# Attention kernel: normalising each head before the output projection, with the softmax denominators inverted on 16 lanes and spread by transfers

## The reference, cut to what matters

```
q, k, v = qkv[0], qkv[1], qkv[2]            # (b, h, n, 64), q scaled by 64 ** -0.5
sim  = einsum('bhid,bhjd->bhij', q, k)      # causal mask on sim
attn = softmax(sim, axis=-1)
out  = einsum('bhij,bhjd->bhid', attn, v)   # (b, h, n, 64)
out  = transpose(out, (0, 2, 1, 3)).reshape(b, n, 16 * 64)
return out @ w_out                          # w_out: (1024, 128)
```

## Time and profile before

| | us |
|---|---|
| median of 3 runs | 1583.55 (1583.36 to 1583.85) |
| the profiled execution | 1578.72 |
| its span, first to last instruction | 1577.0 |
| PE busy | 1453.9 (92%) |
| DVE busy | 1076.1 (68%) |
| ACT busy | 1067.4 (68%) |
| POOL busy | 904.9 (57%) |
| granted TensorE clock, mean | 0.968 |

### The profile page before, as it was taken

One profiled execution on the slowest core, in us unless ns is written; L12 is line 12 of the kernel. 1 busy time (PEld: TensorE's weight loads), 2 busy tenths in 40 slices (PEclk: granted clock), 3 DMA queues, 4 the chain that ended last, 5 costly groups with the idle time before them and its releaser, 6 DMA issues.

```text
span 1577.0 us, 33357 instructions
## 1 busy us (share of the span) xinstructions
PE 1453.9 (92%) x9130; PEld 1128.0 (72%) x9131; DVE 1076.1 (68%) x2341; ACT 1067.4 (68%) x2590; POOL 904.9 (57%) x923
## 2 busy tenths in 40 slices
PE   3569999599999999999999999999999999999998
PEld 3458888477777777777777777777777777777776
DVE  6655555458866876687658776876687668766883
ACT  2536656277776777777767777777777777777775
POOL 0761000167665766676657666766676667666766
PEclk9669999699999999999999999999999999999999
DMA  8122111111111111111111111111111111111111
GB/s 308 48 83 72 52 58 48 40 38 38 33 28 41 38 33 28 41 38 33 28 39 40 33 28 39 40 33 28 39 40 33 28 40 39 33 28 41 37 28 54
DMA packets 58807, 72.86 MB, mean 46 GB/s; under 512 B 7400, under 2 KB 44560, under 8 KB 58640
## 3 DMA queue, kind: packets, MB, share of 16 engines
q1 hardware_dynamic: 40720, 52.57, 14.0%
q10 hardware_dynamic: 13824, 9.86, 2.0%
q0 software_dynamic: 4096, 8.40, 1.8%
HBM read 20.47 MB, written 16.52 MB: 23 GB/s over the span
## 4 chain that ended last, share of the span: by engine, by line
PE 67%; DVE 6%; issue 4%; ACT 3%; DMA 1%; SPq 0%; DVEq 0%; POOLq 0%; POOL 0%; ACTq 0%
PE max_ps L1291 9%; PE score_ps L1316 8%; PE score_ps L1317 8%; PE misc_ps L1350 8%; PE head_ps L1333 7%; PE head_ps L1337 7%; PE head_ps L1335 7%; PE misc_ps L1267 3%; PE max_ps L1294 2%; PE score_ps L1319 2%; DVE q_a L1125 2%; PE misc_ps L1261 2%; ACT p_hi L1082 1%; PE misc_ps L1300 1%; PE misc_ps L1263 1%
## 5 line engine op out<-in xcount | busy, mean ns | idle before, releaser
L1033 POOL TENSOR_TENSOR p_lo<-probs,p_hi 128x512 fp32r<-128x512 f32 (+3 forms) x768 | 773.7, 1022 | 432.0 <-ACT p_hi L1082 426.2
L1082 ACT ACTIVATE probs<-score_ps 128x512 f32<-128x512 f32 (+3 forms) x768 | 375.3, 489 | 250.8 <-PE score_ps L1319 170.9
L1135 DVE TENSOR_REDUCE row_max<-max_ps 128x1 f32<-128x128 f32 (+7 forms) x512 | 386.8, 756 | 171.6 <-PE max_ps L1294 161.0
L1082 ACT ACTIVATE p_hi<-score_ps 128x512 fp32r<-128x512 f32 (+3 forms) x768 | 373.1, 486 | 0.0
L1333 PE MATMUL head_ps<-p_hi,v_hi 128*65 128x512 f32 (+3 forms) x768 | 295.6, 385 | 0.3 <-POOL p_lo L1033 0.3
L1316 PE MATMUL score_ps<-q_a,k_a 128*128 128x512 f32 (+3 forms) x768 | 267.8, 349 | 14.0 <-issue 10.9
L1317 PE MATMUL score_ps<-q_b,k_b 65*128 65x512 f32 (+3 forms) x768 | 267.3, 348 | 0.0
L1291 PE MATMUL max_ps<-k_a,q_a 128*128 128x384 f32 (+5 forms) x768 | 250.1, 380 | 16.4 <-DVE row_max L1135 12.6
L1337 PE MATMUL head_ps<-p_lo,v_hi 128*65 128x512 f32 (+3 forms) x768 | 259.4, 338 | 0.0
L1335 PE MATMUL head_ps<-p_hi,v_lo 128*64 128x512 f32 (+3 forms) x768 | 259.0, 337 | 0.0
L1316 PEld LDWEIGHTS score_ps<-q_a,k_a 128*128 128x128 f32 x768 | 145.4, 189 | 60.0 <-issue 17.4
(11 more groups left out here) (170 smaller groups left out, 2105.6 us busy)
## 6 DMA issues: line engine op xcount, KB each, us to landing
k_a<-k_a SPq DMA_DIRECT2D x64, 256.0 KB, 3.8
q_b<-q_a SPq DMA_DIRECT2D x64, 256.0 KB, 4.3
sorted_x<-zeros SPq DMA_DIRECT2D x13, 384.0 KB, 16.1
w_raw<-sorted_x SPq DMA_DIRECT2D x26, 192.0 KB, 2.5
sorted_y<-result ACTq DMA_DIRECT2D x78, 64.0 KB, 1.6
acc<-in_L_attn_x_dram SPq DMA_DIRECT2D x4, 512.0 KB, 6.9
w_raw<-in_L_ffn_W_dram ACTq DMA_DIRECT2D x1, 2048.0 KB, 23.1
q_b<-shift SPq DMA_DIRECT2D x128, 2.0 KB
```

The lines of the kernel that those rows point to most:

```text
L1033: pool.tensor_tensor(p_lo[:, slot, 0:w], probs[:, slot, 0:w], p_hi[:, slot, 0:w].bitcast(F32), ALU.subtract).then_inc(p_split, 1)
L1082: ins = act.activation(p[:, (g * CH + c) % RING, 0:width], score_ps[(g * CH + c) % 2][:, 0:width], ACT.Exp, scale=SCALE)
L1135: dve.tensor_reduce(row_max[:, g % 2, t:t + 1], src, axes, ALU.max).then_inc(max_taken, 1)
```

## The change

Each head is now normalised before the output product, so that the two heads of a pair can share one product with 128 rows, and the denominator need not be carried through it. For each half of each group there is a chain (`CHAIN`, the numbers are chunks after the half's last chunk):

1. ACT copies `head_ps` to `raw` (65 rows by 512), as it did to `heads`, and now waits that the same half of the group before has been normalised.
2. `fold`, 5 chunks after: SP moves the denominator row of 512 into `den`, 16 lanes by 32.
3. `invert`, 7 after: DVE takes the reciprocal of `den` into `inv`.
4. `store`, 8 after: SP writes `inv` to `inv_rows` in HBM.
5. `spread`, 10 after: SP waits for that, and reads `inv_rows` into 64 lanes by 512 (`scale`).
6. `normalise`, 12 after: DVE multiplies `raw` by `scale` into the 64 rows of `heads` that belong to this head.

In chunks of the group this is: for a half that ended at chunk 3, `fold` at 8, `invert` at 10, `store` at 11, then `spread` at 1 and `normalise` at 3 of the next group; for one that ended at chunk 11, all in the next group, `fold` at 4, `invert` at 6, `store` at 7, `spread` at 9, `normalise` at 11.

The output product of a batch has two units of four tiles, Y0 at chunk 6 of the even group after the pair and Y1 at chunk 1 of the odd one after that. DVE adds a unit in one instruction. The ring of `probs` has 4 slots instead of 6, so ACT waits also for the subtraction four chunks back. `CUT` is 14 instead of 11. The memsets of the ones and zeros in `wo` are gone.

```diff
@@ planning
-            Y_AT = [6, 9, 10]
-            y_units = [(0, 3), (3, 3), (6, 2)]
-            CUT = 11
+            CHAIN = [("fold", 5), ("invert", 7), ("store", 8), ("spread", 10), ("normalise", 12)]
+            Y_AT = {(0, 6): 0, (1, 1): 1}
+            CUT = 14
...
-                if g and g < final and c in Y_AT:
-                    order.append(("y", g - 1, Y_AT.index(c)))
-                    order.append(("add", g - 1, Y_AT.index(c)))
+                if g >= 2 and g < final and (g % 2, c) in Y_AT:
+                    order.append(("y", g // 2 - 1, Y_AT[g % 2, c]))
+                    order.append(("add", g // 2 - 1, Y_AT[g % 2, c]))
...
+                for kind, lag in CHAIN:
+                    if at >= lag and (at - lag) // CH < final and (at - lag) % CH in LAST:
+                        order.append((kind, (at - lag) // CH, LAST.index((at - lag) % CH)))
@@ sync
+                        sp.wait_ge(raw_out, n_half(hp, g, half) + 1)
+                        sp.dma_start(den[:, half], raw[HEAD:HEAD + 1, half].rearrange("o (f n) -> o f n", f=FOLD)
+                                     ).then_inc(den_folded[half], 16)
...
+                        sp.wait_ge(inverted, n_half(hp, g, half) + 1)
+                        sp.dma_start(inv_rows[half].rearrange("(f n) -> f n", f=FOLD), inv[:, half]
+                                     ).then_inc(inv_stored[half], 16)
...
+                        sp.wait_ge(inv_stored[half], hp * (16 * G) + (16 * g + 16))
+                        sp.dma_start(scale[:, half], inv_rows[half].partition_broadcast(HEAD)
+                                     ).then_inc(scale_spread[half], 16)
@@ scalar
+                                if order is not before_loop or g * CH + c >= PROBS:
+                                    act.wait_ge(p_split, n_chunk(hp, g, c) - PROBS + 1)
...
-                                act.activation(heads[:, g % 2, cols], head_ps[0:HEAD + 1, cols],
-                                               ACT.Copy).then_inc(heads_out[half], 1)
+                                act.wait_ge(normalised, n_half(hp, g, half) + 1)
+                                act.activation(raw[:, half], head_ps[0:HEAD + 1, cols],
+                                               ACT.Copy).then_inc(raw_out, 1)
@@ vector
-                        dve.reciprocal(rden[:, u % 2, 0:tiles], src[:, :, D]).then_inc(recip_done, 1)
...
-                        for t in range(tiles):
-                            row = acc[:, g // 2 * TILES + t0 + t]
-                            ins = dve.scalar_tensor_tensor(out=row, in0=src[:, t, 0:D], scalar=rden[:, u % 2, t:t + 1],
-                                                           in1=row, op0=ALU.mult, op1=ALU.add)
-                        ins.then_inc(y_added, 1)
+                    def invert(hp, g, half):
+                        dve.wait_ge(den_folded[half], hp * (16 * G) + (16 * g + 16))
+                        dve.reciprocal(inv[:, half], den[:, half]).then_inc(inverted, 1)
...
+                        dve.wait_ge(scale_spread[half], hp * (16 * G) + (16 * g + 16))
+                        dve.tensor_tensor(heads[s * HEAD:(s + 1) * HEAD, i, cols], raw[0:HEAD, half], scale[:, half],
+                                          ALU.mult).then_inc(normalised, 1)
...
+                        dve.tensor_tensor(acc[:, toks], misc_ps[u % 2][:].rearrange("p (t d) -> p t d", t=GROUP),
+                                          acc[:, toks], ALU.add).then_inc(y_added, 1)
@@ tensor
-                        for t in range(tiles):
-                            q0 = (t0 + t) * P
-                            ins = pe.matmul(dst[:, t * (D + 1):(t + 1) * (D + 1)], heads[:, g % 2, q0:q0 + P],
-                                            wo[:, g % 2], start=True, stop=True)
+                        pe.wait_ge(normalised, n_half(hp, 2 * p + 1, n) + 3)
...
+                        for t in range(GROUP):
+                            q0 = (n * GROUP + t) * P
+                            ins = pe.matmul(dst[:, t * D:(t + 1) * D], heads[:, p % 2, q0:q0 + P], wo[:],
+                                            start=True, stop=True)
```

More of the change, by code:

```diff
@@ L756, in attention_and_experts @@
         pv_done = sem("pv_done")
-        heads_out = [sem(f"heads_out{i}") for i in range(2)]
-        recip_done = sem("recip_done")
+        raw_out = sem("raw_out")
+        den_folded = [sem(f"den_folded{i}") for i in range(2)]
+        inverted = sem("inverted")
+        inv_stored = [sem(f"inv_stored{i}") for i in range(2)]
+        scale_spread = [sem(f"scale_spread{i}") for i in range(2)]
+        normalised = sem("normalised")
         y_added = sem("y_added")
@@ L903, in plan @@
                 order = []
-                for at in range(CUT, G * CH + (LAG if last else CUT)):
+                for at in range(CUT, G * CH + CUT):
                     order += beside(at // CH, at % CH, last)
                 if last:
-                    order += [(kind, G - 1, n) for n in range(len(y_units)) for kind in ("y", "add")]
+                    order += [(kind, BATCH - 1, n) for n in range(2) for kind in ("y", "add")]
                 return numbered(order, MISC0)
@@ L981, in walk @@
                                 qkv_weights(sp, hp + 1)
-                            if o[0] == "y" and o[1:3] == (G - 1, len(y_units) - 1) and not last:
+                            if o[0] == "fold":
+                                fold_denominator(hp, o[1], o[2])
+                            if o[0] == "store":
+                                store_inverse(hp, o[1], o[2])
+                            if o[0] == "spread":
+                                spread_inverse(hp, o[1], o[2])
+                            if o[0] == "y" and o[1:3] == (BATCH - 1, 1) and not last:
                                 sp.wait_ge(misc_ready, n_misc(hp, o[3]) + 1)
@@ L1080, in walk @@
                                 act.wait_ge(pv_done, n_chunk(hp, g, c) + 1)
-                                for p in (probs, p_hi):
-                                    ins = act.activation(p[:, (g * CH + c) % RING, 0:width],
+                                if order is not before_loop or g * CH + c >= PROBS:
+                                    act.wait_ge(p_split, n_chunk(hp, g, c) - PROBS + 1)
+                                for p, ring in ((probs, PROBS), (p_hi, RING)):
+                                    ins = act.activation(p[:, (g * CH + c) % ring, 0:width],
                                                          score_ps[(g * CH + c) % 2][:, 0:width], ACT.Exp,
@@ L1366, in walk @@
                             elif kind == "pv":
-                                values(hp, g, c)
+                                values(hp, g, c, order is not before_loop)
                             elif kind == "y":
```

82 lines of the change are left out of this document (40 added, 42 removed).

## The result

The changed kernel takes 1688.6 us (median; 1683.3 to 1693.1), the kernel before 1583.7: a ratio of 1.066, with a 95% interval of 1.062 to 1.069. It is slower, as forecast, but by 105 us and not by 26. The profiled execution has a span of 1688.7 us against 1577.0.

A forecast was written before the change was run, and what follows sets the result against it. PE, busy 92% of the span, was taken to set the time. Terms -54 + 54 + 21 + 5 = +26 us gave 1605 us profiled, 1610 for the median; the 8-in-10 range was 1567 to 1636.

The forecast's parts named there:

- What PE is spared: Output products on PE: 64 units of four tiles at 0.86 us replace 109 us of work, a gain of 54 us.
- the bound of 0.95: Output product on PE: upper bound in us for a four-tile unit, taken from P4; the gain would be 48 us.
- Chunk 1 of odd groups: S1 goes 1.8 us late behind the transfers, normalise and v_lo, at 30 places: 54 us lost.
- the forecast's clock: Time in us counted from 0 at the first score of chunk 6 of the even group before.
- A sign that I had named: On DVE: if the forecast is right, DVE waits for den at chunk 10 of even groups only.
- After odd groups ... the reductions behind it have slack: Without copies the chain comes about 2 us earlier and only meets POOL; reductions have slack, so no cost outside three places a pass.
- The clock should stay, since PE has no pause of many us: PE throughout: the granted clock was expected not to fall, so no cost was counted.
- Other places: Combine steps of groups 3 and 5, gathers of groups 1 and 2: 21 us, between 0 and 42.
- a meeting with POOL: DVE held by one POOL subtraction, priced at 0.87 us in each of three places a pass.
- The tail: From the last heads copy to the last store's issue: 8.0 to 9.2 us instead of 3.9, +5 us.
- As work I cost this at nothing: DVE's added reciprocals and products: room in the mean (68% busy), so 0 us.
- The rivals: Transfers in time: 1576 us, chance 0.15; others covered too: 1555, 0.10; loses twice: 1634, 0.17; half the places hit: 1584, 0.08.

The follow-up runs named there:

- e13: Changed kernel with later chain, half 0's normalisation at chunk 9, a second raw for half 0, later Y units, combination steps at their old places: 1579.7 us, ratio 0.998.
- e4: Changed kernel with the four 256 KB copies issued by ACT instead of SP: 1727.8 us, ratio 1.092.
- e2: Changed kernel with invert, store, spread and normalise later (8, 9, 11, 14), Y0 at chunk 8 and Y1 at chunk 3: 1606.1 us, ratio 1.015.
- e1: Changed kernel without the three transfers; DVE inverts and multiplies constants, so output isn't normalised: 1614.5 us, ratio 1.020.
- e7: Kernel before the change, with TensorE held at chunk 1 of every odd group for an unused 1900-column reduction on DVE: 1763.4 us, ratio 1.116.
- e9: Kernel before the change, with TensorE held at chunk 1 of every group for an unused 128-column reduction on DVE: 1780.7 us, ratio 1.125.
- e10: As e2, with half 0's normalisation at chunk 4 of the next group, its spread one chunk earlier, and combination steps behind the reductions: 1609.6 us, ratio 1.017.
- e12: As e2, with half 0's normalisation at chunk 9, a second raw for half 0, Y0 at chunk 10, three combination steps moved: 1612.5 us, ratio 1.018.

## Why the prediction was wrong by 79 us

**What PE is spared: 54 us forecast, 43 measured.** By the forecast's own measure, from the start of one product to the start of the next, the output projection took 109.6 us before and 58.9 in e13. That is 0.92 us for a unit, between the 0.86 that I took and the bound of 0.95, and a gain of 51. Active time fell by only 43. The other 8 us are in the row-maximum and score products, by the same measure 453 us before and 461 in e13; 57 of them follow a pause there, 20 before, with nothing in front to overlap. That this is the reason is argued, not shown.

**Chunk 1 of odd groups: the place and the price were right** (52 us against 54), and e4 confirms that the store behind the copies holds Y1. The way to the price was not; that they agree is luck. Medians over the 30 places, on the forecast's clock: the store was issued at 5.7, as I had it. The spread was issued at 8.85 instead of 8.35, and `normalise` began 2.7 to 3.9 us after it, where I had taken 2.3: at 12.15, not 10.65. But then it met no subtraction of POOL in 19 of the 30 places and took 0.69, where I had reckoned it waiting for POOL until 11.66 (in the other 11 it took 0.75 to 1.3). And P4 ended at 11.4, not 10.97, so less of the delay was left to wait for. Lost on the transfers 1.5 us, gained back 1.0 and 0.4. A sign that I had named failed as well: DVE waited for `den` not only at chunk 10 of even groups but in 11 odd groups too.

**"After odd groups ... the reductions behind it have slack": this step failed, 32 us.** The store is earlier there, as I wrote, but so is everything that needs DVE: half 1's chain lies 12 chunks behind in every group. I looked at the reductions and forgot P0's subtraction, although had shown S1 waiting for just that, with no slack at all, before the change. e2 gives the 32 us back and e1 most of them. More than half of the loss is in group 2 of the passes, for which I had only the gathers in mind.

**"The clock should stay, since PE has no pause of many us": this step failed, 40 us.** Pauses of about 2 us were enough, 60 of them with a mean of 1.6 us. e7 to e9 show it without the change, and e13, whose waits are 1.4 us or less but for six at the loop's branch and the tail, shows it gone. The trace before had the warning: two of its six pauses at the loop's branch, of 2.1 and 1.8 us, were followed by a fall. I should have put a bound there.

**Other places: 21 us forecast, 24 measured** (17 at the row maxima, 7 at the branch, for which the forecast had 0, within 5). e1 has them nearly whole, so they come from DVE's work and not from the transfers. Pricing a meeting with POOL at one subtraction held in this kernel, but not in e1, where it cost 5 us in each pass. **The tail: +5 forecast, +6 measured.** **"As work I cost this at nothing"** was true of the mean alone: e2, e10 and e12 each found a stretch in which DVE's queue had no gap, and each cost 22 to 35 us; e13 still waits 34 us more for DVE than the kernel before.

Together: 11 us of gain that wasn't there, 32 in even groups, 40 by the clock, 3 in other places and 1 at the tail, less 2 in odd groups, are 85. The profiled executions miss the forecast's 1605 by just that (1690.5); the medians, 1688.6 against 1610, by 79.

The rivals were all built around odd groups. None let both kinds of group lose, so the range ended 53 us short of the result.

## What to carry to other kernels

Before a step is put on an in-order queue, walk every place of its period and list what is queued behind it there; a wait that the profile already shows, however small, marks a place with no slack, and anything put ahead of it is paid in full. Count a regularly repeated pause of TensorE of some 2 us or more at one and a half times its length (1.35 to 1.75 times here), and look at the granted clock of the stretch behind it. When moving one step moves the wait instead of ending it, look at the full list of waits and not only at the one that was to go: here the change as written and seven rearrangements of it cost 1.5 to 9%, and an eighth was 0.2% faster than leaving it out.

## What the runs showed that I had not expected

- Short pauses lower TensorE's clock: in e9, with pauses of 1.8 and 2.8 us, it stood at 1.2 GHz for 156 us in the attention, against 14 in the kernel before. Over the attention of all 15 traces (the start and the tail left out), a fall began within 6 us of the start of 181 of the 184 pauses of 2.5 us or more, of 84 of the 161 between 1.75 and 2.5, of 9 of the 77 between 1.5 and 1.75, and of 4 of the 563 between 0.5 and 1.5. Longer pauses are the surer ones, and no sharp limit shows.
- Not only `normalise` is held by POOL's subtraction. `TENSOR_SCALAR` on 128 x 128, with one tensor input in SBUF, takes 0.33 us alone and 3.91 for four beside POOL (e12). The Trainium skill ("SBUF — State Buffer", "Who interferes with whom") names `tensor_scalar` among the operations that can take the shared pair of ports; the trace agrees.
- Issuing is not free of its queue: S0's transfer on SP took 1.25 us in the middle behind four copies, in both kernels, and about 0.6 without them (the 2.04 in the timeline above is the longest of all). Four copies on ACT cost more there (e4) than all that they had held up on SP.
- One `normalise` on DVE stood for the length of four subtractions of POOL in a row, 5.5 us, where POOL had a backlog (e1).
- Inverting 32 columns took 0.33 us on DVE; the store of 2 KB that follows it landed after 1.3 to 3.5 us, with a median of 2.4.
